# A cross-attention kernel's first stage: the last token softmax ahead of the first norm's rounding, extra TensorE products during the first loads, and one load semaphore for each self-attention weight

## The reference, cut to what matters

```
# adapter: 8 heads of 20
hs     = mha(x @ Wq, enc @ Wk, enc @ Wv)            # 512 queries on 73 context rows
ca_q1  = (ca^T @ Wq_ca)                             # 96 rows, later repeated to 512
ca_hs1 = mha(ca_q1, x, x)                           # 96 queries on the 512 rows of x
ca_hs2 = mha(ca_hs1 @ Wq, ca @ Wk_ca, ca @ Wv_ca)   # softmax over 4 tokens: "token softmax"
x      = (hs + repeat(ca_hs2)) @ Wout + b_out + x
# transformer block: 20 heads of 64
x = self_attention(layer_norm(x)) + x
x = cross_attention(layer_norm(x), context) + x
x = geglu_ff(layer_norm(x)) + x
```

## Time and profile before

| | us |
|---|---|
| median of 3 timed runs | 1027.56 (1027.3 to 1028.69) |
| the profiled execution, device time | 1029.73 |
| its span, first to last instruction | 1027.9 |
| mean granted TensorE clock over the span | 0.995 |

### The profile page before, as it was taken

How to read it: one execution, slowest core, us unless ns; L and a number is a source line. 1 busy time by engine, 2 the same in 40 slices (tenths; PEclk the granted TensorE clock), 3 DMA queues, 4 the chain that set the end, 5 groups by cost and what they waited for, 6 DMA issues and landing times.

```text
span 1027.9 us, 17534 instructions
## 1 busy us (share of the span) xinstructions
PE 978.5 (95%) x6376; PEld 706.1 (69%) x6376; DVE 690.7 (67%) x1171; ACT 591.1 (57%) x1332; POOL 378.9 (37%) x493
## 2 busy tenths in 40 slices
PE   7999978999999999999999999999999989999998
PEld 4566666656667666667666668666556689998887
DVE  2767646776774676774777674776645789999463
ACT  2666635667763766764666764666644455455442
POOL 2676623344342434332444332343321034444120
PEclk9999989999999999999999999999999999999999
DMA  6400050000000000000000000000000330000000
GB/s 135 94 1 1 1 148 1 1 1 2 1 1 2 1 1 2 1 1 1 1 1 2 1 1 2 1 1 2 1 1 25 100 95 1 1 1 1 1 26 26
DMA packets 25371, 17.64 MB, mean 17 GB/s; under 512 B 8566, under 2 KB 24102, under 8 KB 25286
## 3 DMA queue, kind: packets, MB, share of 16 engines
q1 hardware_dynamic: 25285, 16.52, 6.4%
HBM read 11.26 MB, written 1.31 MB: 12 GB/s over the span
## 4 chain that ended last, share of the span: by engine, by line
PE 64%; DVE 10%; ACT 5%; issue 4%; POOL 1%; DMA 1%; SPq 0%; DVEq 0%; ACTq 0%; POOLq 0%
PE banks L409 13%; PE banks L396 12%; PE banks L382 11%; PE banks L416 4%; PE banks L224 3%; ACT sa_probs L499 3%; PE banks L1645 2%; PE banks L227 2%; PE banks L226 2%; PE banks L225 2%; PE banks L1937 2%; DVE ca_top L1780 2%; PE banks L232 2%; DVE ca_probs L1785 1%; DVE sa_negmax L571 1%
## 5 line engine op out<-in xcount | busy, mean ns | idle before, releaser
L643 POOL TENSOR_SCALAR sa_probs<-sa_probs,sa_inverse 128x512 f32<-128x512 f32 x320 | 216.8, 692 | 361.7 <-DVE sa_inverse L575 361.7
L499 ACT ACTIVATE sa_probs<-banks,sa_negmax 128x512 f32<-128x512 f32 x320 | 215.6, 685 | 125.7 <-DVE sa_negmax L571 125.6
L571 DVE TENSOR_REDUCE sa_negmax<-banks 128x2 f32<-128x1024 f32 x160 | 188.7, 1218 | 10.4 <-PE banks L382 7.4
L396 PEld LDWEIGHTS banks<-ident,sa_probs 128*128 128x128 f32 x1280 | 144.5, 141 | 55.6 <-issue 27.6
L396 PE MATMUL banks<-ident,sa_probs 128*128 128x128 f32 x1280 | 172.6, 275 | 9.9 <-ACT sa_turned L510 5.8
L580 DVE COPY sa_turned<-banks 128x512 f32<-128x512 f32 x160 | 110.1, 688 | 75.6 <-PE banks L396 75.6
L409 PE MATMUL banks<-sa_turned,sa_v 128*64 128x512 f32 x640 | 155.0, 605 | 0.0
L382 PE MATMUL banks<-sa_k_parts,sa_q_parts 64*128 64x512 f32 x960 | 133.2, 408 | 1.9 <-ACT sa_probs L499 1.9
L510 ACT COPY sa_turned<-banks 128x512 f32<-128x512 f32 x160 | 94.2, 589 | 58.2 <-PE banks L396 56.3
L382 PEld LDWEIGHTS banks<-sa_k_parts,sa_q_parts 64*128 64x128 f32 x960 | 83.9, 184 | 30.4 <-issue 14.1
L409 PEld LDWEIGHTS banks<-sa_turned,sa_v 128*64 128x64 f32 x640 | 38.7, 136 | 74.3 <-issue 73.1
(11 more groups left out here) (218 smaller groups left out, 1727.2 us busy)
## 6 DMA issues: line engine op xcount, KB each, us to landing
w_o<-in_L_xattn_wo SPq DMA_DIRECT2D x2, 800.0 KB, 9.1
out<-x SPq DMA_DIRECT2D x4, 320.0 KB, 2.4
w_q_t<-in_L_xattn_wq_t SPq DMA_DIRECT2D x1, 1120.0 KB, 10.4
fold_values<-ca_turned SPq DMA_DIRECT2D x5, 192.5 KB
x<-in_x SPq DMA_DIRECT2D x1, 960.0 KB, 5.8
fold_values<-ca_probs SPq DMA_DIRECT2D x4, 192.5 KB
w_q_t<-in_L_xattn_wq SPq DMA_DIRECT2D x1, 640.0 KB, 6.2
w_o<-in_L_xattn_wk SPq DMA_DIRECT2D x1, 640.0 KB, 9.2
```

The source lines that it names most:

```text
L396: last = pe.transpose(b_turn[e][:, q * P:(q + 1) * P], probs[:, j % 2, e, q, k * P:(k + 1) * P], ident[:])
L499: act.activation(probs[:, j % 2, e, q, :], b_scores[u % 2][:, e, :], ACT.Exp, bias=negmax[:, u % RING, e:e + 1], accum_out=total[:, u % RI ...
L571: dve.tensor_reduce(negmax[:, u % RING, :], b_scores[u % 2], AX_X, ALU.max, negate=True).then_inc(s_max.sem, 1)
L643: pool.tensor_scalar(probs[:, j % 2, e, q, :], probs[:, j % 2, e, q, :], inverse[:, u % RING, e:e + 1], 1.0, ALU.mult, ALU.mult).then_inc( ...
```

## The change

Three things are done. (1) In the tail, for the last batch only, `exp2` goes ahead of the norm's scaling on ScalarE, `copy_expanded` between its scaling and its rounding; `expand_probs2` goes ahead of output product 11 on TensorE; VectorE's `remainder` goes from slot 17 to the end of slot 18, behind `shift2`, `finish2` and `update(11)`. (2) TensorE makes 5, 4 and 2 products of a 128x128 tile of ones with itself, whose results nobody reads (`b_out` is free then): before the wait for the identity, after turning the context, and after turning the first batch of x. (3) Each self-attention weight has its own load semaphore.

```diff
+        busy = sb("busy", [P, P])
+        s_raw = [ctx.enter_context(nc.semaphore(f"ad_raw{i}_loaded")) for i in range(len(splits))]
+        s_busy = ctx.enter_context(nc.semaphore("ad_busy_tile_set"))
# sync
-            for (weight, parts), raw in zip(splits, raws):
-                parts.load(sp, weight, raw, s_raw)
+            for (weight, parts), raw, loaded in zip(splits, raws, s_raw):
+                parts.load(sp, weight, raw, loaded)
# tensor
+            def keep_busy(n):
+                for _ in range(n):
+                    pe.matmul(b_out[:, 0:P], busy[:], busy[:], start=True, stop=True)
+
+            pe.wait_ge(s_busy, 1)
+            keep_busy(5)
             pe.wait_ge(s_ident, 16)
             pe.wait_ge(s_ctx, 32)
             for b in range(B):
                 last = pe.transpose(b_token[0:CTX, b * SK:(b + 1) * SK], context[:, b, :], ident[0:SK, 0:SK])
             last.then_inc(s_cturn.sem, 1)
+            keep_busy(4)
             for g in range(G):
                 turn_x(0, g)
+            keep_busy(2)
             pe.wait_ge(s_w, 16 * N_W)
...
+                if s == NU + 2:
+                    expand_probs2(B - 1)
                 if 0 <= s - OUT_LAG < NU - 3:
                     project_out(s - OUT_LAG)
...
-                if k == 2 and 1 <= b <= B:
+                if k == 2 and 1 <= b < B:
                     expand_probs2(b - 1)
# scalar (exp2 and copy_expanded in the slots get the same `b < B`)
-                    act.wait_ge(s_raw, 16 * Split.LOADS * len(splits))
+                    act.wait_ge(s_raw[i], 16 * Split.LOADS)
...
                 if s == NU + 1:
+                    exp2(B - 1)
                     act.wait_ge(s_later, 16 * len(later))
-                    next_ln.scale_and_round(act, 0, banks[0:2], lambda eng: None)
+                    next_ln.scale(act, 0, banks[0:2])
+                    copy_expanded(B - 1)
+                    next_ln.round(act, 0, lambda eng: None)
# vector
-                if s == NU + 1:
+                if s == NU + 2:
                     next_ln.remainder(dve, 0, lambda eng: None)
# gpsimd
+            pool.memset(busy[:], 1.0).then_inc(s_busy, 1)
             next_ln.start_gpsimd(pool)
```

More of the change, by code:

```diff
@@ L793, in adapter @@
         out_of = lambda u: out_banks.get(u, b_out)[:, OUT:OUT + D]
-        s_ident, s_in, s_xrest, s_w, s_wq, s_wo, s_raw, s_later, s_last, s_ctx = (ctx.enter_context(nc.semaphore(f"ad_{n}_loaded")) for n in
-            ("ident", "first_x", "other_x", "weights", "wq", "out_weights", "raw", "later", "last", "context"))
+        s_ident, s_in, s_xrest, s_w, s_wq, s_wo, s_later, s_last, s_ctx = (ctx.enter_context(nc.semaphore(f"ad_{n}_loaded")) for n in
+            ("ident", "first_x", "other_x", "weights", "wq", "out_weights", "later", "last", "context"))
+        s_raw = [ctx.enter_context(nc.semaphore(f"ad_raw{i}_loaded")) for i in range(len(splits))]
+        s_busy = ctx.enter_context(nc.semaphore("ad_busy_tile_set"))
         s_zero = ctx.enter_context(nc.semaphore("ad_cleared"))
```

## The result

The changed kernel takes 1020.52 us (median of 4 runs, 1020.31 to 1021.72) against 1027.72 us in the same comparison: 0.9931 of the time, 95% interval 0.9914 to 0.9948. The forecast was 1017.9 with a range of 1015.8 to 1022.9. The profiled execution took 1020.68 us, span 1018.9.

What follows compares the result with a forecast made beforehand. TensorE, with 64% of the chain, was taken as the bound, so gains come from its waits and lower clock. Tail 5.4 plus setup 4.3, semaphores 0: 1027.6 - 9.7 = 1017.9 us, range 1015.8 to 1022.9.

Steps and rivals of the forecast that it cites:

- The sum's 1.52: Tail: each of output products 12 to 15 at the full clock level, four needing 6.1 us.
- 1.5 us moved, not added: Tail, TensorE: output product 11, now behind expand_probs2, runs 144.5 to 146.0 instead of 142.62 to 144.14.
- Sum 5.9, less the delay: Setup: what a risen clock saves on lines 1033, 1039 to 1041, 915, queries and values, less the fillers' delay.
- the limit that the sum had: Setup: the rest of x lets turn_x(1) start at 19.65 against 24.70, at most 5.05 us gained.
- rival (c): Handover between the blocks: the clock falls behind TensorE's 2.0 us idle, plus 1.7 us, time 1019.6; chance 0.15.
- would come at 36.2 and wait up to 2.4 for it: ScalarE's first rounding, with the setup 4.3 us shorter, would wait for wv's last load without the separate semaphores.
- both parts at their most: Range's lower end, 1015.8: tail at most 5.8, setup at most 5.05, with a quiet handover.
- (a): Setup: transposes between fillers make the clock rise late; front gains 1.0 instead of 4.3, time 1021.2; chance 0.17.
- (b): Setup: the fillers do not help and only delay; front minus 0.8, time 1023.0; chance 0.10.
- (d): Tail clock falls although the stall is gone (gain 0.5), fillers delay setup by 0.9; time 1028.0; chance 0.03.

Runs made afterwards that it cites:

- hand_expand: more_hand with expand_probs2(3) put back behind output product 11 on TensorE, rest of the new tail kept; 1017.94 us, 0.9909.
- front_only: The changed kernel with the tail's old order back; extra products and three semaphores stay; 1025.29 us, 0.9979.
- one_sem: The changed kernel with all twelve self-attention weight loads on one semaphore again; 1021.50 us, 0.9933.
- more_fill: The changed kernel with 7 instead of 2 extra products ahead of the small weights' wait and 6 more behind the key projections; 1018.21 us, 0.9905.
- tail_only: The changed kernel without its 11 extra products; tail order and three semaphores stay; 1023.36 us, 0.9954.
- gap_one: more_fill without the 6 products behind the key projections; 1021.02 us, 0.9934.
- late_fill: The changed kernel without the five products ahead of the identity's landing; the later 4 and 2 stay; 1021.77 us, 0.9934.
- late_turn: As late_fill, but the extra products are transposes of the identity, 7 after turning the context and 3 after turning x; 1022.41 us, 0.9943.
- more_hand: more_fill plus 4 products of the identity with itself as TensorE's first instructions of the second block; 1016.92 us, 0.9895.
- hand_one_sem: more_hand with all twelve self-attention weight loads on one semaphore again; 1017.16 us, 0.9913.

## Why the prediction was right, and where it was off

**The tail** was right in mechanism and size: 5.4 forecast, 2.8 from the stall and 2.6 from the clock. The sum's 1.52 for an output product at the full level is 157.27 + 0.43 - 156.18 in the earlier trace rows, and the clock that the forecast wins back is the 0.50 from 148.1 to 154.9 in the earlier trace rows. It came out as 5.53 in the trace, of which product 12 starts 2.75 closer to `scores2` and the four products take 2.78 less. The chain ended at 140.19, 1.39 us behind `scores2` (I had 1.35 plus the handing over), `remainder` was covered, and no window between the expansion and the last product is below 1.00 (1.00 from 140.2 to 149.2). I called the place of `expand_probs2` ahead of product 11 "1.5 us moved, not added"; hand_expand shows that it left 0.5 on the table; TensorE idles 0.56 before the expansion and 0.57 before product 12, where hand_expand has one idle of 0.87.

**The setup** was right in direction and too large: 4.3 forecast, 3.06 in the trace. The 0.43 that it saves on each of four query passes is by the earlier trace rows: one weight load and the idle before it are 0.34 + 0.52 = 0.86 at 21.31 and 0.19 + 0.24 = 0.43 at 22.42, so the clock was low until about 21.8. The step that failed is "Sum 5.9, less the delay": it prices line 915 and all query passes at the high level, that is, it takes for granted that a clock once risen stays. It rose earlier than I had it (4.7 us) and fell at 11.5. I first laid that to the idle of 1.1 us, and front_only shows the same fall at 12.0 with no idle at all, while TensorE made line 1045's and the key products. The earlier trace rows had the warning: the same products kept TensorE busy from 8.57 to about 15.3 and did not raise the clock, and I priced them as if they would hold it. Nor was the rise at 4.7 typical: it came at 7.6 in one_sem, with the same TensorE instructions, and the setup gained only 24.70 - 23.34 = 1.36 there. I had listed the falls in the tail and at the handover as rivals, and not the one in the setup, although the wait for the small weights and VectorE's 1.38 us stood in my own sum. more_fill, with both holes filled, starts the slots another 2.06 us earlier, a gain of 5.12 in all, and ran into the second load of x at 19.58, the limit that the sum had (19.65 and 5.05). The price of the extra products was right: 2.50 us for the first five, all hidden.

**The handover** was rival (c), with a chance of 0.15: it came true in the profiled execution, and the means of the other three (0.995 or 0.993) fit it without proving it. Its price, 1.7 forecast, is 8.65 - 7.09 = 1.56 by the distance of the two traces' line 232 (165.16 and 158.07), and 0.9 by the split of tail_only's executions. I gave it too little weight because the same 1.99 us had done nothing in the trace of before. The traces sort by the order of the tail: the clock fell behind the handover in all seven with the new order and nothing put into the idle (the change, tail_only, one_sem, more_fill, gap_one, late_fill, late_turn; windows at 0.50 begin at 151.5, 156.7, 154.4, 149.4, 153.9, 154.1 and 156.2), and in neither with the old order, the kernel before and front_only (idles of 1.99 and 1.90, and 1.00 from 157.8 to 949.0 and from 152.0 to 1020.0). So the tail's new order gave part of its gain back there. tail_only's two executions at 1.000 show that it need not happen, and why the order matters stays open.

**The semaphores** protect nothing in the changed kernel's trace, and kept a wait away in more_hand's, where the last load landed 3.0 us behind the first rounding. Failed: "would come at 36.2 and wait up to 2.4 for it", which took one landing time of one execution as fixed.

**The sum.** Forecast 9.7, measured 7.2: 1.2 less in the setup and 1.5 lost in the handover are 2.7, near the 2.5 that are missing. The range's lower end was mis-added: both parts at their most, 5.8 and 5.05, give 1027.6 - 10.85 = 1016.75, not 1015.8. The remaining rivals: (a) and (b) did not occur in the profiled execution, whose setup gained 3.06, at the low end of the forecast's 3 to 5; one_sem's 1.36 is as much as (a) had, by another way. (d) did not occur.

## What to carry to other kernels

A clock that filler work has raised need not stay (up at 4.7 and down at 11.5 in the change): list what TensorE does up to the dense part, waits and thin products alike, before pricing a rise. A row in which the same work ran at the low clock without raising it (here 8.57 to 15.3) is a reason not to price that work at the high one. In the setup, seven products instead of two at the first wait brought nothing by themselves, and with six more at the second wait 2.3 us. Sequencer work at the head of a block was a place for such products at no cost (first projection 1.94 us behind the last product with them, 1.93 without). A wait for loads is priced by their landing in several traces, since one trace gives one value of a wide spread (10.6 to 15.9 us for the slowest of line 260's loads). Where a stall is removed, look at what stands in order between its source and its end: the gain was in the order of three engines' lists, and half of it (2.78 of 5.53) was the clock that the stall had cost.

## What the runs showed of the hardware

- A window of the profile prints a granted clock of 1.00 before the first recorded change, while query passes take 0.86 instead of 0.43 us (before about 21.8 us; late_turn's line 1049 takes 2.92 instead of the 1.55 of late_fill's line 1044). In a setup, go by durations.
- The same kernel's executions differ in their mean clock: tail_only 0.998 or 1.000 (0.9 us apart), late_turn 0.993, 0.998 or 1.000 (1024.25 at 0.998, 1022.41 and 1022.51 at 1.000). One profile shows one of these. The change and one_sem give TensorE the same instructions, and the clock rose at 4.7 in one trace and at 7.6 in the other.
- The slowest of line 260's loads in the setup landed 10.6 (hand_one_sem), 11.5 (the change), 13.1 (more_fill), 13.8 (one_sem), 14.6 (before), 14.8 (more_hand) and 15.9 us (tail_only) after its issue.
- The granted clock fell to 0.50 behind an idle of 1.38 us (gap_one) and of 1.93 us (the handover, in the change and in more_fill), and stayed at 1.00 behind one of 0.69 (more_hand), the tail's two of 0.57, and the handover's 1.99 and 1.90 with the old tail (before, front_only), in the executions profiled. It also fell with no idle, at 12.0 in front_only, behind 3.3 us of products of 4 rows and key projections.
